# Gated delta attention and a feed-forward layer on one core: weights loaded once per group of heads, 32x32 blocks moved through DRAM, four places for k

## The reference

```
x = x + layernorm(attention(layernorm(x)))
x = x + layernorm(ffn(layernorm(x)))

attention: 32 heads of 64 (keys) by 64 (values)
  q, k, v, z = split(h @ w_qkvz.T);   b, a = split(h @ w_ba.T)
  q, k, v    = causal convolution with 4 taps, per channel
  g = -exp(A_log) * softplus(a + dt_bias);   beta = sigmoid(b)
  q = l2norm(q) / 8;   k = l2norm(k)
  for each token t:  S = S * exp(g_t)
                     delta = (v_t - k_t S) * beta_t
                     S = S + outer(k_t, delta);   o_t = q_t S
  o = o * rsqrt(mean(o*o) + eps) * norm_weight * sigmoid(z);   return o @ w_out.T
ffn: silu(h @ w_gate.T) * (h @ w_up.T) @ w_down.T,  inner width 1024
```

## Time and profile before

| | |
|---|---|
| median of 3 runs | 3615.0 us (3611.3 to 3629.6) |
| profiled execution, own time | 3628.4 us |
| its span | 3626.6 us |
| mean granted TensorE clock over the span | 0.961 of full speed |
| busy: PE, DVE, ACT, POOL | 91%, 69%, 49%, 30% |
| data moved by DMA | 351 MB, mean 97 GB/s, 930,158 packets, 857,712 of them under 512 bytes |

### The profile page before, as it was taken

One profiled execution on the slowest core, in us unless ns is written; L12 is line 12 of the kernel. 1 busy time (PEld: TensorE's weight loads), 2 busy tenths in 40 slices (PEclk: granted clock), 3 DMA queues, 4 the chain that ended last, 5 costly groups with the idle time before them and its releaser, 6 DMA issues. The chain is left out here.

```text
span 3626.6 us, 117234 instructions
## 1 busy us (share of the span) xinstructions
PE 3284.2 (91%) x51008; PEld 2221.8 (61%) x51008; DVE 2486.1 (69%) x5826; ACT 1769.1 (49%) x3338; POOL 1093.2 (30%) x902
## 2 busy tenths in 40 slices
PE   4489999999999999999999999999999999869998
PEld 2246666666666666666666666666666666645554
DVE  5467767777777777777777777776776777635555
ACT  2245555555555555555555545554555555423333
POOL 0043333333333333333333333333333333300000
PEclk7689999999999999999999999999999999969999
DMA  2235445444544444444444444444444454320000
GB/s 76 75 91 112 113 112 113 113 113 113 113 113 104 103 108 108 106 104 112 104 113 113 113 113 113 113 113 103 110 113 91 109 115 98 87 71 18 24 24 18
DMA packets 930158, 351.24 MB, mean 97 GB/s; under 512 B 857712, under 2 KB 878576, under 8 KB 921328
## 3 DMA queue, kind: packets, MB, share of 16 engines
q1 hardware_dynamic: 929648, 343.73, 40.3%
HBM read 240.35 MB, written 61.34 MB: 83 GB/s over the span
## 5 line engine op out<-in xcount | busy, mean ns | idle before, releaser
L1134 PE MATMUL bank<-xT,w_sb 128*128 128x512 f32 x2048 | 1023.0, 623 | 22.0 <-DMA w_sb<-in_w_qkvz 17.5
L678 POOL TENSOR_TENSOR kq<-kq,products 128x510 f32<-128x510 f32 (+2 forms) x384 | 445.0, 1165 | 941.9 <-ACT kq L752 656.6
L1134 PEld LDWEIGHTS bank<-xT,w_sb 128*128 128x128 f32 x2048 | 350.3, 190 | 309.5 <-issue 253.6
L930 DVE SCALAR_TENSOR_TENSOR kq<-bank,cw,kq 128x510 f32<-128x510 f32 (+2 forms) x384 | 286.6, 746 | 203.9 <-ACT kq L752 189.3
L666 POOL TENSOR_TENSOR dec_a<-gcrow,gccol 128x1024 f32<-128x1024 f32 x64 | 121.8, 1904 | 1001.1 <-DMA beta<-beta_d 1001.1
L1162 PE MATMUL bank<-kq 64*64 64x128 f32 x4096 | 280.7, 278 | 13.2 <-issue 11.4
L930 DVE SCALAR_TENSOR_TENSOR v_c<-bank,cw,v_c 128x510 f32<-128x510 f32 (+2 forms) x384 | 285.2, 743 | 9.0
L948 DVE TENSOR_TENSOR x_un<-x_un,prod_un 128x15 f32<-128x15 f32 (+7 forms) x960 | 258.1, 269 | 32.9
L944 DVE TENSOR_TENSOR prod_un<-a_un,x_un 128x15 f32<-128x15 f32 (+7 forms) x960 | 255.8, 266 | 29.9 <-DMA a_un<-a_d 3.3
L1255 PE MATMUL bank<-wo,u_sq 128*128 128x256 f32 x1024 | 261.4, 399 | 2.8 <-DVE u_sq L1007 2.8
L1162 PEld LDWEIGHTS bank<-kq 64*64 64x64 f32 x4096 | 237.2, 137 | 19.1 <-issue 19.1
(11 more groups left out here) (135 smaller groups left out, 6148.2 us busy)
## 6 DMA issues: line engine op xcount, KB each, us to landing
w_sb<-in_w_qkvz SPq DMA_DIRECT2D x64, 1024.0 KB, 7.9
xT<-xT_d SPq DMA_DIRECT2D x64, 512.0 KB, 5.4
gcrow<-gcrow_d SPq DMA_DIRECT2D x128, 256.0 KB, 5.5
a_d<-a_mat SPq DMA_DIRECT2D x128, 256.0 KB, 3.9
k_old<-kq SPq DMA_DIRECT2D x64, 512.0 KB, 3.8
z_t<-z_d SPq DMA_DIRECT2D x128, 256.0 KB, 4.6
x_row<-x_d SPq DMA_DIRECT2D x128, 256.0 KB, 4.5
wo<-in_w_out SPq DMA_DIRECT2D x64, 256.0 KB, 3.2
```

Of the source, the lines that this page charges most:

```text
L678: nc.gpsimd.tensor_tensor(t[:, :, d:SEQ], t[:, :, d:SEQ], prod[:, :, 0:SEQ - d], ALU.add).then_inc(tap_added[i], 1)
L930: ins = nc.vector.scalar_tensor_tensor(t[:, :, d:SEQ], src[:, :, 0:SEQ - d], cw[:, w:w + 1], t[:, :, d:SEQ], ALU.mult, ALU.add)
L1134: ins = nc.tensor.matmul(bank[:, :], w_sb[:, h, s * P:(s + 1) * P], xT[:, h, :], start=(h == 0), stop=(h == HT - 1))
```

## The change

- **Weights.** `w_sb`, `cw` and `wo` have two buffers each, indexed by the group's parity (`m.grp % 2`), and are loaded once for the 8 steps of a group, by `weights(g)`: for group 0 at the first step, for group g+1 when x of the seventh step of group g has been sent. The activation `scale_wo` runs once per group. `xT` has two buffers and its load waits for nothing.
- **k.** `kq` becomes one tile with six places: k of a step lies in place `m.off % 4`, q in place `4 + m.par`. `keep_k`, `k_old` and the waits on `k_old_in` are gone; `key_state` reads `kq`.
- **Blocks.** DRAM holds 32x32 blocks: for each of the four quarters of the partitions (32 rows) the block on the diagonal. `units_out`, `z_back` and `x_back` each issue four DMAs of a quarter; a row is 32 elements (128 bytes), in `x_back` only the upper left 16x16 (64 bytes). `units_in`, `z_out` and `x_out` issue one DMA in place of two, `x_out` only for every second block. What isn't moved is zero in `z_t` and `x_row` from memsets on POOL in stage 1, and only z_d is set to zero in DRAM.
- **Gates.** gccol and beta lie in one tile `gcb` and come by one DMA.
- The order of work in the turns of PE, ACT, DVE and POOL is kept.

```diff
-    MAT = C * C + C
+    MAT = W2 * W2 + W2
...
+        def rows32(t, q):
+            return t[q].rearrange("(g x) -> g x", x=MAT)[:, 0:W2 * W2].rearrange("g (i c) -> i g c", c=W2)
+        def blocks16(t):
+            return t.rearrange("q x -> (q x)").rearrange("(u x) -> u x", x=MAT // 2)[:, 0:B * W2] \
+                .rearrange("u (i c) -> u i c", c=W2)[:, :, 0:B]
...
-        xT = sb("xT", [P, HT, TB])
-        w_sb = sb("w_sb", [P, HT, 8 * P])
-        cw = sb("cw", [P, 6 * TAPS])
+        xT = [sb(f"xT{i}", [P, HT, TB]) for i in range(2)]
+        w_two = [sb(f"w_sb{i}", [P, HT, 8 * P]) for i in range(2)]
+        w_sb = w_two[0]
+        cw_two = [sb(f"cw{i}", [P, 6 * TAPS]) for i in range(2)]
-        kq = [sb(f"kq{i}", [P, 2, PAIRS, TB]) for i in range(2)]
+        kq = sb("kq", [P, 6, PAIRS, TB])
-        k_old = [sb(f"k_old{i}", [P, G, C]) for i in range(2)]
...
-                    for h in range(2):
-                        zero = z_t[0][D * h:D * h + D, :, :]
-                        sp.dma_start(whole(z_d, h), zero).then_inc(zeros_out, 16)
-                        sp.dma_start(whole(x_d, h), zero).then_inc(zeros_out, 16)
+                    for q in range(4):
+                        sp.dma_start(rows32(z_d, q), z_t[0][W2 * q:W2 * q + W2, :, 0:W2]).then_inc(zeros_out, 16)
...
+            def half_of(m, q):
+                return kq[:, 4 + m.par if q else m.off % 4, :, :]
...
+                    def weights(g):
+                        if g > 1:
+                            for k in range(2):
+                                sp.wait_ge(op_full[k], NSP * (g - 1))
+                        sp.dma_start(w_two[g % 2]..., w_qkvz[g]).then_inc(w_in, 16)
+                        sp.dma_start(cw_two[g % 2][:, :], conv_w[g]).then_inc(cw_in, 16)
+                        sp.dma_start(wo[g % 2]..., w_out[g]).then_inc(wo_in, 16)
+                    def load_x(m):
+                        sp.dma_start(xT[m.par]..., xT_d[m.index() % NSP]).then_inc(x_T_in[m.par], 16)
+                        if m.off == 0:
+                            weights(0)
+                        if m.off % NSP == NSP - 2 and m.grp + 1 < NHG:
+                            weights(m.grp + 1)
...
                     def units_out(m):
+                        for q in range(4):
+                            c = W2 * (q % 2)
+                            sp.dma_start(rows32(a_d, q), a_mat[m.par][W2 * q:W2 * q + W2, :, c:c + W2]).then_inc(a_d_out, 16)
                     def units_in(m):
+                        sp.dma_start(a_un[:, :, :], blocks16(a_d)).then_inc(a_un_in, 16)
                     def z_out(m):
+                        sp.dma_start(blocks16(z_d), t_un[:, :, :]).then_inc(z_d_out, 16)
                     def z_back(m):
+                        for q in range(4):
+                            c = W2 * (q % 2)
+                            sp.dma_start(z_t[m.par][W2 * q:W2 * q + W2, :, c:c + W2], rows32(z_d, q)).then_inc(z_in, 16)
                     def x_out(m):
+                        sp.dma_start(blocks16(x_d)[0::2], x_un[0::2, :, :]).then_inc(x_d_out, 16)
                     def x_back(m):
+                        for q in range(4):
+                            c = W2 * (q % 2)
+                            sp.dma_start(x_row[W2 * q:W2 * q + B, :, c:c + B], rows32(x_d, q)[0:B, :, 0:B]).then_inc(x_row_in, 16)
...
                         if s[1]:
-                            wait_for(sp, proj_full[7], s[1], 1, back=1)
-                            load_xw(s[1])
+                            load_x(s[1])
```

More of the change, by code:

```diff
@@ L67, in gated_delta_sandwich @@
         gcrow_d = scratch("gcrow_d", [NHG, PAIRS, 2, NSP, TB])
[L68 to L79, removed]
+        gcb_d = scratch("gcb_d", [NHG, NSP, P, 2, G])
+        a_d, z_d, x_d = (scratch(n, [4, G * MAT]) for n in ("a_d", "z_d", "x_d"))
+        def rows32(t, q):
[3 more added lines that the diff above has]
+                .rearrange("u (i c) -> u i c", c=W2)[:, :, 0:B]
         ident = sb("ident", [P, P])
@@ L278, in _ @@
                     nc.gpsimd.memset(z_t[0][:, :, :], 0.0).then_inc(zeros, 1)
+                    nc.gpsimd.memset(z_t[1][:, :, :], 0.0).then_inc(zeros, 1)
+                    nc.gpsimd.memset(x_row[:, :, :], 0.0).then_inc(zeros, 1)
                     nc.gpsimd.memset(acc[:, :, :], 0.0)
@@ L544, in gated_delta_sandwich @@
             vtok_full = {i: sem2(f"vtok_full{i}") for i in (0, 1,)}
-            wo_in = sem2("wo_in")
+            x_T_in = [sem2(f"x_T_in{i}") for i in range(2)]
             x_d_out = sem2("x_d_out")
@@ L560, in gated_delta_sandwich @@
             zt_done = sem2("zt_done")
-            act_self, dve_self, pe_gate2 = sem2("act_self"), sem2("dve_self"), sem2("pe_gate2")
+            act_self, dve_self, pe_gate2, w_in, cw_in, wo_in, wo_done = (
+                sem2(n) for n in ("act_self", "dve_self", "pe_gate2", "w_in", "cw_in", "wo_in", "wo_done"))
             def grp(t, c):
                 return t[:, :, :].rearrange("p (a c) j -> p a c j", c=NCH)[:, :, c, :]
+            def half_of(m, q):
+                return kq[:, 4 + m.par if q else m.off % 4, :, :]
             def col(t):
@@ L750, in first_tap @@
                     def first_tap(m, s, bank):
[L751 to L752 removed]
+                        dst = v_c[:, s - 4, :] if s >= 4 else half_of(m, s // 2)[:, s % 2, :]
+                        if m.off % NSP == 0:
+                            act.wait_ge(cw_in, 16 * m.grp + 16)
+                        ins = nc.scalar.activation(dst, bank[:, :], ACT.Identity, scale=cw_two[m.grp % 2][:, s * TAPS + TAPS - 1:s * TAPS + TAPS])
                         if s in tap_done:
@@ L821, in turn @@
                         if s[1]:
-                            wait_for(act, cw_in, s[1], 16)
-                            wait_for(act, k_old_in, s[1], 16, back=2)
                             wait_for(act, proj_full[1], s[1], 1)
@@ L891, in turn @@
                         if s[2]:
-                            wait_for(act, wo_in, s[2], 16)
-                            scale_wo(s[2])
                             wait_for(act, p16_full, s[2], 1)
@@ L1252, in project_out @@
                     def project_out(m, k, bank):
+                        if m.off % NSP == 0:
+                            pe.wait_ge(wo_done, m.grp + 1)
                         for t in range(2):
```

124 lines of the change are left out of this document (47 added, 77 removed).

## The result

| | before | changed |
|---|---|---|
| median of 4 runs each, us | 3622.3 (3611.3 to 3630.7) | 3481.4 (3477.4 to 3483.4) |
| profiled execution, us | 3628.4 | 3480.0 |
| its span, us | 3626.6 | 3477.9 |
| mean granted TensorE clock | 0.961 | 0.975 |
| first solve of step 0 to that of step 62, us | 2907.7 | 2774.8 |

The ratio of the medians is 0.961, interval 0.958 to 0.965: 3.9% faster, some 141 us. The forecast was 3500 us with a range of 3468 to 3560.

What follows compares the result with a forecast made beforehand. PE was taken as the bound, losing time to late instruction blocks and a slow clock. Terms 63.5 + 6 + 11 + 32 + 2 = 114.5 us off 3628.4 gave 3514, less 13.4 to the median: 3500 us, range 3468 to 3560.

Steps and rivals of the forecast that it cites:

- What bounds the kernel: Attention stage: PE bounds, 94% busy; 96.7 us of issue gaps, read as instruction blocks queued behind data, plus half-clock stretches.
- The stops: PE's issue gaps: 63.5 us at L1182 and L1162 all go, 6 in small groups, 11 at L1200.
- small groups: Eight small sets of PE issue gaps, 10.4 us in all, the largest L1173 with 2.7; 6 us go.
- the turns in which weights go out: Seven turns where the old burst is back: up to 3 us each, 10 us of the bound.
- The clock: PE's half-clock stretches after long stops: between 0 and 44 us to win, 32 taken; first and last turns keep theirs.
- The start: Zeros written on SP's path before the attention stage fall from 1,024 KB to 256: 2 us.
- What was costed at nothing: Fewer scale_wo activations on ACT, waits removed, new waits on weights, gates behind four issues of a_d: each 0 us.
- SP from z_out on: SP's four issues each for z_t and x_row, 0.65 us apiece: in time by 0.9 and 1.8 us, costing nothing.
- rival 3: Four issues too slow: z_t and x_row land late, PE stops 2.1 us in each turn, 3663 us; chance 0.06.
- z_t's 128-byte runs: Load of z_t in the burst after z_out: 1.3 us by bytes, 2.7 by runs, 2.0 taken.
- Rival 1: Instruction supply to PE is late whatever the data do: only the zeros go, 3613 us, no change; chance 0.08.
- Rival 2: Runs, not bytes, fill the DMA engines: L1200 stays, half the clock loss stays, 3530 or 3546 us; with mixtures 0.23.

Runs made afterwards that it cites:

- the pair with equal bytes: Changed kernel with w_sb sent in every turn again, right behind xT (3543.0 us) or, the same bytes, behind units_in (3471.2 us).
- The three parts alone: Kernel before with one part each: weights once per group 3564.1 us, 32x32 blocks 3584.3 us, six places in kq without k_old 3590.2 us.

## Why the prediction was right, and where it wasn't

**What bounds the kernel** was read rightly in the main. Instructions that come late made most of the gaps of L1182, L1162 and L1200: they follow a count of instructions and end with the arrival of a packet, and the pair with equal bytes shows that it is the place of a burst in PE's list that costs. Two things were wrong or missing. 7.1 of the 52.1 us at L1182 were x_row landing late, not instructions; they went with the same burst, so the term didn't suffer, which is luck. And a stop needs a late packet *and* a stretch of PE's list with small matmuls; nothing in the prediction asked how fast PE uses up a block.

**The stops.** Forecast: 63.5 us at L1182 and L1162, 6 in small groups and 11 at L1200, together 80.5; the rows of the waits fell by 83.8. The parts differ more than the sum. L1182 and L1162 keep 3.5 and 1.7 of 63.5. L1200 kept 4.3 of 22.8, where half was forecast to stay: the price of a_d's writes fell further than their share of bytes led me to expect. The other groups keep 3.4 of 10.4, most of it one gap of 2.2 at L1168. In the prediction, 10 us stood as a bound for the turns in which weights go out. Those seven turns exceed the usual 44.4 by 4.0, 1.1, 1.3, 1.6, 1.8, 0.1 and 1.7 us, 11.6 in all.

But a stop costs more than its row says. The row counts idle time from the modelled end of the last matmul, and in these groups records of 0.2 us start every 0.03 us, so most of one record's length is missing from it. Both kernels have the same 47,844 records between the first solve of step 0 and that of step 62. Set against each other from start to start, they split the 132.9 us that the 62 turns gave into 94.4 at stops, 36.0 in the stretches at half clock and 2.5 elsewhere. So the stops were worth 94.4 in place of 80.5.

**The clock** was the other term that came out too small. Forecast 32 us, as the stage's ends would keep their share. Within the 62 turns the granted clock stood at 0.50 for 85.3 us before (21 stretches) and for 6.8 after (2 stretches), 42.7 and 3.4 us of full-speed time; the bound of 44 was well read, and 36.0 of it came in. The tail, forecast at nothing, gave another 11.5 us (470.2 from the first solve of step 62 to the end of the span, now 458.7). It is clock nearly all of it, by the same count. The windows from that solve on, before:

```profile
3156.00:3200.00 44.00, 30.99 (x565) 25.52 (x566) 16.42 (x50) 13.03 (x26) 0.00 (x0) 0.70 0.26 53
3200.00:3250.00 50.00, 28.59 (x298) 21.67 (x298) 18.92 (x48) 6.53 (x16) 0.00 (x0) 0.64 0.23 85
```

and after:

```profile
3019.00:3063.00 44.00, 31.97 (x628) 26.79 (x628) 19.18 (x56) 13.22 (x26) 0.00 (x0) 0.84 0.13 16
3063.00:3113.00 50.00, 28.25 (x256) 18.02 (x257) 16.79 (x45) 8.24 (x18) 0.00 (x0) 0.80 0.23 85
```

PE is busy for about as long in the two windows together, but at 0.84 and 0.80 of its clock rather than 0.70 and 0.64, and gets through more (884 records in place of 863). So the clock gave 47 to 48 us in place of 32. Why it falls less at the stage's end was not tried by itself.

**The start** gave 4.3 us, forecast 2 for the zeros: the first solve came at 248.74 and comes at 244.40. 3.9 of it show at one wait, PE's for the first w_sb, 17.5 us before and 13.6 now.

**The sum.** The three pieces, 132.9 + 11.5 + 4.3 = 148.7, are the difference of the spans. The prediction's sum was 114.5, 34 short of it: 14 at the stops, 15.5 at the clock, 2.3 at the start, 2.5 elsewhere. By the medians, 3500 against 3481, it is 19 short. The difference is the step from one execution to the median: I took off 13.4 us, but the changed kernel's profiled execution lies 1.4 us below its median. That step was wrong and hid 15 us of the miss; that the forecast looks this close is partly luck.

**What was costed at nothing** cost nothing: `scale_wo`, the waits taken away and the new ones, the gates. Neither w_in nor wo_done stands among PE's waits in the turns, and no load of cw or wo among ACT's.

**SP from z_out on** was right in sign and wrong in size. I had z_t in time by 0.9 us and called the cover thin; it is in time by about 4.5. An issue takes 0.48 us, not 0.65, and the landing 2.5, not 4.6 (these DMAs are also a quarter of the size, 64 KB in place of 256). Both prices were taken from a kernel whose queue was full. The queue that the change empties seems to make each of its own steps cheaper too, so rival 3 (it would have decided at 1.4 us per issue) was never near, and 0.06 for it was enough.

**z_t's 128-byte runs.** I took 2.0 us, between 1.3 by bytes and 2.7 by runs. The window in which they alone move shows share 0.64 at 101 GB/s:

```profile
1658.00:1659.00 1.00, 1.00 (x41) 1.00 (x39) 1.00 (x3) 0.56 (x2) 1.00 (x1) 1.00 0.64 101
```

That is 158 GB/s at full share, and 256 KB take 1.7 us: between the two, nearer to bytes.

**The rivals.** Rival 1 (supply late whatever the data do) falls. The Trainium skill ("DMA: Bandwidth & Descriptors", Queues, rings and completion order) has the engines take turns packet by packet. The traces agree in so far as a packet of instructions, once begun, isn't slow: median 1.00 us before and 1.04 after. The late thing is its start, and the time isn't what that rule alone would make it. What remains of rival 1 is small: gaps of up to 0.7 us at L1195, 4.3 us in all, that stay even where the loads were moved away (3.1). Rival 2 (runs count, not bytes) falls in its strong form: 19% fewer packets took 39% less engine time. Taking it as a price per run would have left L1200 at 22.8 us; it came to 4.3.

**The range** of 3468 to 3560 had 60 us above the forecast and 32 below, and the result used 19 of those below. Three terms of the sum had been cut ("6 of 10.4", "32 of 44", "half of 22.8"), all in the same direction, and all too deep.

## What to carry to other kernels

Where a dense stream of small matmuls stops in the middle of a group with no semaphore between and the DMA engines full, ask first whether the burst can be sent under long matmuls: moving w's load by 16 us within a turn was worth 72 us, more than leaving it out at its old place was (62 us, from 3543.0 to 3481.4). Before giving an engine's instruction an earlier place to end a wait, look in the lists of the engines that follow it for what stands in front of the next link: here the wait moved from DVE to ACT and grew, until ACT's order was changed as well. And issue and landing times read from a crowded queue can be too high for a change that empties it. Where "issue" ends a wait at the head of a group, look at the landing of the DMA that the group waits for before calling it anything else.

## What was not expected of the hardware

- A burst that fills the DMA engines for 6 us cost PE nothing under matmuls of 128x512 and 128x256, and 1 to 3 us under small ones (64x128 and 64x32): 68 and 124 records used in 6 and 4 us.
- PE may stand after the burst is over: 1.50 us with a share of 0.23 in the window 1602 to 1604 above. The block comes later than the engines come free, here 1.46 us after its packet had ended.
- Eight semaphore increments in a row in PE's stream cost 0.56 us a turn at the next matmul, 34.1 us in 61 turns.
- The three parts alone gave 128 us and together 141; the blocks gave 38 us alone and 61 on top of the other two. With fewer bytes in the way, what is left is worth more, not less. The runs don't tell why; the spread of the kernels with stops (3536 to 3554 for one of them, 3477 to 3483 for the changed kernel) is a part of it at most.
